# Attention values and row sums of two steps taken together at odd steps, in a fused macaron layer on eight cores

## What is computed

```python
x = x + 0.5 * ffn(layernorm(x))
x = x + attention(layernorm(x))      # 16 heads of 64, causal
x = x + 0.5 * ffn(layernorm(x))
```

```python
q = (x @ Wq.T + bq); k = (x @ Wk.T + bk); v = (x @ Wv.T + bv)
att = softmax(where(causal, q @ k.T / 8, -inf))
y = (att @ v) @ Wp.T + bp
```

## Time and profile before

| what | us |
|---|---|
| median of the runs shown | 1458.96 |
| the profiled execution | 1457.06 |
| its span, slowest core (core 4) | 1455.3 |
| spans of the 8 cores | 1439.4 to 1455.3 |
| TensorE busy (matmul) | 1227.4 |
| VectorE, ScalarE, GpSimd busy | 800.4, 712.0, 436.3 |

### The profile page before, as it was taken

The page is one execution under the profiler, slowest core; times in us unless marked ns, Lnnn a source line. Parts: engine busy times, 40 slices in busy tenths (PEclk is TensorE's granted clock), DMA queues, the critical chain, the costliest instruction groups (busy, mean ns, idle before and its releaser), DMA issues.

```text
span 1455.3 us, 27013 instructions; the slowest of 8 cores (1439.4 to 1455.3 us)
## 1 busy us (share of the span) xinstructions
PE 1227.4 (84%) x8256; PEld 475.0 (33%) x8392; DVE 800.4 (55%) x1469; ACT 712.0 (49%) x865; POOL 436.3 (30%) x308
## 2 busy tenths in 40 slices
PE   0338788879989999999999999966989799998977
PEld 0124333423333333333333333322333333333333
DVE  4466757646745745644654654425655445555545
ACT  0004335045646566566666566644646465565600
POOL 2012504503502412321340433324243232523222
PEclk9969999989999999999999999988999999999988
DMA  6828935146134324433433254243243343433132
GB/s 188 273 74 266 293 116 166 48 130 189 45 105 127 125 70 152 131 95 105 134 104 105 80 138 125 88 142 116 84 149 117 123 147 137 153 129 126 68 114 87
DMA packets 125929, 187.92 MB, mean 129 GB/s; under 512 B 45536, under 2 KB 90592, under 8 KB 125792
## 3 DMA queue, kind: packets, MB, share of 16 engines
q1 hardware_dynamic: 125792, 186.20, 40.3%
HBM read 119.05 MB, written 67.11 MB: 128 GB/s over the span
## 4 chain that ended last, share of the span: by engine, by line
PE 70%; DVE 10%; DMA 8%; issue 7%; ACT 2%; POOL 1%; SPq 1%; DVEq 0%; ACTq 0%; POOLq 0%
PE PS L689 14%; PE PS L702 13%; PE PS L619 10%; PE PS L638 10%; PE PS L744 7%; PE PS L712 7%; PE PS L646 6%; PE PS L667 3%; DMA WQKV<-x1d 2%; DVE XN L791 1%; DMA ATT<-wte 1%; DVE BNS L761 1%; DMA WQKV<-od 1%; PE PS L733 1%; DVE XT L807 1%
## 5 line engine op out<-in xcount | busy, mean ns | idle before, releaser
L930 ACT ACTIVATE PT<-PS,MB 128x1024 bf16<-128x1024 f32 (+3 forms) x428 | 401.3, 989 | 245.4 <-PE PS L619 245.4
L689 PE MATMUL PS<-WF,XT 128*128 128x512 bf16 x982 | 239.1, 391 | 31.2 <-DVE GD L813 23.5
L930 ACT ACTIVATE ATT<-PS,MB 128x1024 bf16<-128x1024 f32 x212 | 193.8, 965 | 123.3 <-PE PS L619 123.3
L702 PE MATMUL PS<-XT,WQKV 128*128 128x512 bf16 x979 | 233.5, 382 | 17.2 <-DVE QKS L847 7.5
L489 POOL TENSOR_TENSOR SQ<-QKS 128x512 bf16<-128x512 bf16 x128 | 143.9, 1127 | 291.0 <-DVE QKS L847 221.3
L619 PE MATMUL PS<-ATT 64*128 64x512 bf16 (+3 forms) x1280 | 185.6, 354 | 28.8 <-DMA ATT<-vd 17.1
L496 POOL TENSOR_TENSOR OTT<-OS,RR 128x512 bf16<-128x512 f32 x64 | 84.7, 1324 | 389.0 <-ACT RR L942 389.0
L744 PE MATMUL PS<-WP,WQKV 128*128 128x512 bf16 x490 | 126.0, 405 | 28.7 <-DMA WQKV<-od 18.0
L689 PEld LDWEIGHTS PS<-WF,XT 128*128 128x128 bf16 x1024 | 94.7, 100 | 151.2 <-issue 58.7
L702 PEld LDWEIGHTS PS<-XT,WQKV 128*128 128x128 bf16 x1024 | 91.8, 98 | 130.3 <-issue 36.4
L667 PE MATMUL PS<-IDE,XN 128*128 128x128 bf16 x768 | 63.7, 234 | 80.0 <-DVE XN L791 57.8
(11 more groups left out here) (75 smaller groups left out, 1200.8 us busy)
## 6 DMA issues: line engine op xcount, KB each, us to landing
XC<-x SPq DMA_DIRECT2D x32, 512.0 KB, 5.9
x1d<-XC SPq DMA_DIRECT2D x32, 512.0 KB, 4.6
WQKV<-x1d SPq DMA_DIRECT2D x32, 512.0 KB, 5.9
out<-WQKV SPq DMA_DIRECT2D x32, 512.0 KB, 3.3
qd<-QKS SPq DMA_DIRECT2D x64, 128.0 KB, 2.4
kd<-QKS SPq DMA_DIRECT2D x64, 128.0 KB, 2.1
vd<-VST SPq DMA_DIRECT2D x32, 256.0 KB, 2.7
ATT<-qd SPq DMA_DIRECT2D x64, 128.0 KB, 2.5
```

The lines of the kernel that those rows point to most:

```text
L689: m = e.matmul(sbank(en), x[:, dc, t * 128:(t + 1) * 128], WF[:, dc, h * 512:(h + 1) * 512], start=(dc == 0), stop=(dc == DCN - 1))
L702: m = e.matmul(sbank(en), WQKV[:, int(w), dc, hp * 128:(hp + 1) * 128], XT2[:, i % 2, dc, :], start=(dc == 0), stop=(dc == DCN - 1))
L930: e.activation(ptile(k)[:, 2 * m:2 * m + 2, off:512], PS[:, S_BANK + 2 * m:S_BANK + 2 * m + 2, off:512], AF.Exp, bias=MB[:, u // HPN, hp % ...
```

## The change

- `values(k)` works for two steps, k and k+1: eight value products, then eight row-sum products, and counts both at once (`then_inc(p_pv, 2)`). It is called at odd steps alone, behind `scores(k)`, for steps k-3 and k-2 (LAG = 3). Behind the scores of an even step nothing of the attention stands on TensorE.
- There are four buffers of exponentials instead of three: two in `PT`, two behind the ring. The exponential of step k waits for the values of step k-4.
- To make room, the ring shrinks from 10240 to 9216 columns, and the buffer `LNR` goes: the logarithm is written to `RR` and the exponential works there in place. So the wait for GpSimd's product of unit u-2 now stands ahead of the logarithm.
- Loads are entered in the order by what has been finished, and `PRED` follows from the smaller ring.

The core of the diff:

```diff
-LAG = 2
+LAG = 3
...
-RING = 10240
+RING = 9216
...
-        while u < NUNIT and START[u + 1] <= state["avail"] and START[PRED[u] + 1] <= max(0, state["k"] - LAG):
+        while u < NUNIT and START[u + 1] <= state["avail"] and START[PRED[u] + 1] <= state["done"]:
...
-        v = k - LAG
+        v = k - LAG + 1 if k % 2 and k > LAG - 2 else -1
+        if v >= 0:
+            state["done"] = v + 1
...
-            if k % 3 < 2:
-                return PT[:, k % 3, :, :]
-            return ATT[:, RING:RING + 2048].rearrange("p (a f) -> p a f", a=4)
+            if k % 4 < 2:
+                return PT[:, k % 4, :, :]
+            b = RING + 2048 * (k % 4 - 2)
+            return ATT[:, b:b + 2048].rearrange("p (a f) -> p a f", a=4)
...
             def values(k):
-                e.wait_ge(a_ex, 2 * k + 2)
-                if is_diag(k):
-                    e.wait_ge(v_mk, DIAG[k + 1])
+                e.wait_ge(a_ex, 2 * k + 4)
+                if is_diag(k + 1):
+                    e.wait_ge(v_mk, DIAG[k + 2])
                 if j == 0 and u:
                     e.wait_ge(v_oe, u)
-                for m in range(2):
+                for m in range(4):
...
-                                 vv[:, v + 64 * h:v + 64 * h + 64], ptile(k)[:, 2 * m + h, off:512],
+                                 vv[:, (j + m) * 128 + 64 * h:(j + m) * 128 + 64 * h + 64],
+                                 ptile(k + m // 2)[:, 2 * (m % 2) + h, off:512],
...
-                i.then_inc(p_pv, 1)
+                i.then_inc(p_pv, 2)
...
-                    if LAG <= k < NQUAD + LAG:
+                    if k % 2 and LAG <= k < NQUAD + LAG:
                         values(k - LAG)
...
-                        if k > LAG:
-                            e.wait_ge(p_pv, k - LAG)
+                        if k >= 4:
+                            e.wait_ge(p_pv, k - 3)
...
-                    if u:
-                        e.wait_ge(a_rc, u)
-                    was_read(e.activation(LNR[:, :], sbank(en), AF.Ln), en)
-                    read_out(e, en)
                     if u >= 2:
                         e.wait_ge(g_ot, u - 1)
-                    e.activation(RR[:, u % 2, :], LNR[:, :], AF.Exp, scale=-1.0).then_inc(a_rc, 1)
+                    x = RR[:, u % 2, :]
+                    was_read(e.activation(x, sbank(en), AF.Ln), en)
+                    read_out(e, en)
+                    e.activation(x, x, AF.Exp, scale=-1.0).then_inc(a_rc, 1)
```

More of the change, by code:

```diff
@@ L188, in make_order @@
     out = []
-    state = {"k": 0, "avail": 0, "acc": 0.0, "al": 0, "before": 0}
+    state = {"k": 0, "avail": 0, "acc": 0.0, "al": 0, "before": 0, "done": 0}
     def loads():
         u = state["al"]
-        while u < NUNIT and START[u + 1] <= state["avail"] and START[PRED[u] + 1] <= max(0, state["k"] - LAG):
+        while u < NUNIT and START[u + 1] <= state["avail"] and START[PRED[u] + 1] <= state["done"]:
             out.append(("al", u))
@@ L320, in build_program @@
         BD = sb("BD", [128, 2, 32], BF16)
-        ATT = sb("ATT", [128, NST * 2 * D], BF16)
+        ATT = sb("ATT", [128, RING + 4096], BF16)
         PT = sb("PT", [128, 2, 4, 512], BF16)
@@ L325, in build_program @@
         DSB = sb("DSB", [128, 2, 512], BF16)
-        LNR = sb("LNR", [128, 512], F32)
         RR = sb("RR", [128, 2, 512], F32)
@@ L359, in build_program @@
             "p (n m) f -> p n (m f)", n=NXC)
-        STG = ATT[:, :].bitcast(F32).rearrange("p (n f) -> p n f", n=NST)
+        STG = ATT[:, 0:NST * 2 * D].bitcast(F32).rearrange("p (n f) -> p n f", n=NST)
         BST = XT2[:, :, :, :].bitcast(F32).rearrange("p a c f -> p (a c f)").rearrange("p (n f) -> p n f", n=4)
@@ L628, in values @@
                 vv = vtile(u)
-                e.wait_ge(a_ex, 2 * k + 2)
-                if is_diag(k):
-                    e.wait_ge(v_mk, DIAG[k + 1])
+                e.wait_ge(a_ex, 2 * k + 4)
+                if is_diag(k + 1):
+                    e.wait_ge(v_mk, DIAG[k + 2])
                 if j == 0 and u:
                     e.wait_ge(v_oe, u)
-                for m in range(2):
+                for m in range(4):
                     off = k_off(c, j + m)
-                    v = (j + m) * 128
                     for h in range(2):
                         e.matmul(PS[64 * h:64 * h + 64, O_BANK, off:512],
-                                 vv[:, v + 64 * h:v + 64 * h + 64], ptile(k)[:, 2 * m + h, off:512],
+                                 vv[:, (j + m) * 128 + 64 * h:(j + m) * 128 + 64 * h + 64],
+                                 ptile(k + m // 2)[:, 2 * (m % 2) + h, off:512],
                                  start=(j + m == 0), stop=(j + m == end))
-                for m in range(2):
+                for m in range(4):
                     off = k_off(c, j + m)
                     for h in range(2):
-                        g = 2 * h + (m if c else 0)
+                        g = 2 * h + (m % 2 if c else 0)
                         i = e.matmul(PS[32 * g:32 * g + 32, D_BANK, off:512], ONES[:, 0:32],
-                                     ptile(k)[:, 2 * m + h, off:512],
-                                     start=(j == 0 and (m == 0 or c > 0)),
+                                     ptile(k + m // 2)[:, 2 * (m % 2) + h, off:512],
+                                     start=(j == 0 and (m == 0 or c > 0 and m == 1)),
                                      stop=(j + m >= end - (1 if c else 0)))
-                i.then_inc(p_pv, 1)
+                i.then_inc(p_pv, 2)
             for en in ORDER:
```

## The result

The changed kernel takes 1488.63 us (median; the kernel before 1457.01 beside it), 1.0208 times the kernel before, with a 95% interval from 1.0152 to 1.0265. On a later chip the same kernel gave 1.0185 (1.0132 to 1.0238). Each kernel has some runs in which the cores of a die show a lower granted clock and the time is longer (1609.85 and 1609.54 us here); they are in the medians, but not in the ratios and intervals. So the change is slower by about 2%, 27 to 30 us by the two ratios; whether by more or less than 2% the intervals leave open, as the forecast did (0.49 for slower, 0.47 for no change). 1489 us had been forecast. The experiments ran on three chips; the kernel before, which ran beside them each time, had medians of 1456.75 to 1459.96 us there.

A forecast was written before the change was run, and what follows sets the result against it. TensorE was taken to set the pace, with exponentials hidden by little. Terms -29 + 39 + 6 + 10 + 3 + 5 - 5 + 3 = +32 us on 1457 gave 1489 us; range 1463 to 1508, 8 times in 10.

The forecast's parts named there:

- The 45 and 15 steps behind a normaliser (+39, +6): Even steps right behind a unit's normaliser: scores wait for exponentials, 0.87 us at 45 (+39), some 0.4 at 15 (+6).
- Plain steps (+10, +3): Even steps with one projection: waits for exponentials, 0.21 us at 47 (+10), 0.12 at 24 with 384-wide second pair (+3).
- The saved changes of shape (-29): TensorE's values and row sums: 0.88 us removed from even steps, 0.70 added to odd, 0.18 saved a pair, times 160.
- Six steps without projection, and odd steps that fill waits (+5, -5): Values that hid in waits come later at 6 even steps (+5); longer batch fills waits at some 15 odd (-5).
- What was costed at nothing: Four buffers, the logarithm's earlier wait and the smaller ring: 0 us, at most 4 once for unit 48's loads.
- The clock: Rival: new waits bring stretches at a lower TensorE clock, adding 26 us, 1515 us; chance 6 in 100.
- Cover holds: Rival: TensorE never waits at the odd steps, only the saved changes of shape remain, 1428 us; chance 6 in 100.
- Waits half as large: Rival: normaliser steps partly covered by waits on banks and transposes, row sums join at 0.22, 1465 us; chance 25 in 100.
- The joined row sums cost more: Rival: second row-sum set starts only 0.33 us after the first, -29 shrinks by 14, 1503 us; chance 8 in 100.
- the rule on weight loads: Weight loads overlap a running matmul only for another group of rows; by it -29 would become +22, the time 1540.
- a term of 3 us for other steps alone: 23 even steps with more work, no normaliser: projection may reach its bank before VectorE has read it; +3, between 0 and 8.
- a sign of being wrong: The projection behind even scores starting much later than 0.53 us after them.

The follow-up runs named there:

- the first edit: The changed kernel with each unit's broadcast, logarithm and exponential of the normaliser one projection later, ahead of an odd step: 1424.77 us, ratio 0.9776.
- half the dose: The changed kernel with a shorter normaliser in place (logarithm and nearly all of the second exponential left out, layer not computed): 1471.22 us in the profiled execution.
- the move alone: The kernel before, without the change, with the normaliser shifted one projection later: 1461.37 us, ratio 1.0018.
- the late normaliser: The changed kernel with the normaliser one projection later, the same kernel as the first edit: 1424.77 us, ratio 0.9776; on another chip 1438.01 us, ratio 0.9843.
- the values ahead of the scores: The changed kernel with the odd step's batch of values and row sums ahead of its scores, normaliser in place: 1453.54 us, ratio 0.9963.
- the batch undone: The changed kernel with values and row sums of the two steps done one step after the other inside the odd step: 1521.98 us, ratio 1.0419.

## Why the prediction came out right

- **The sum.** +32 us forecast, +27.6 in mean span, +26 in the profiled executions (1482.72 against 1457.06), +30 by the ratio. The mechanism was the one forecast: the time is lost where the exponentials behind a normaliser are no longer covered.
- **The 45 and 15 steps behind a normaliser (+39, +6).** Right in place, mechanism and size. Forecast +2.74 and +3.74 for the two pairs, measured +2.69 and +3.70; the first edit got the time back, half the dose a part of it, and the move alone nothing in the kernel before. Most of the first pair's delay is the bank wait, though, which is not in the forecast of +2.74. The 15 steps shortened less than I had put: 13 us of work was removed and 3.9 us saved, where 7 were expected.
- **Plain steps (+10, +3).** Right. The median length of a plain full step is 2.58 us where scores and projection take 2.37; of one with a 384 wide second pair it is 2.37, where 2.26 would do (the next pair follows 0.11 sooner).
- **The saved changes of shape (-29).** Right in kind, too small. What I put at 0.46 us for two pairs of value products is 0.43 (0.98 against 0.55), the second set of row sums took 0.22, not 0.24, and the projection after scores started after 0.54, as assumed. So 0.88 - 0.65 = 0.23 us a full pair, up to 37 us; undoing the batch cost 33. The 143 odd steps with one projection grew by 93.5 us, which is 0.65 each.
- **Six steps without projection, and odd steps that fill waits (+5, -5).** The first class kept its length to 0.1 us, as said. The second came true too: the 14 odd steps without a projection grew by 4.0 us where 14 times 0.65 is 9.1, so waits took up 5. That the odd steps' sum grew by 10 us less than expected is owed to the term above.
- **What was costed at nothing.** The memory part cost nothing that can be measured, by its own run. Unit 48's last load was issued at 975.87, landed at 980.26 and was used at 984.01, 3.7 us to spare; 1 to 2 had been forecast.
- **The clock.** It was to stay at 1.00 from 560 to 910 us; it was 0.99. An estimate from that is 7 us of 350 at the lower level of 1.2 GHz, which costs at most half as much. Over the whole span the mean of the eight cores went from 0.961 to 0.956, by which at most 8 us of TensorE's time were lost, an estimate too; the late normaliser had 0.959 and 0.954 on its two chips. This rival came true in a small part, a few us:

```profile
619.00:692.00 73.00, 67.02 (x480) 24.77 (x476) 36.04 (x72) 43.62 (x51) 16.86 (x11) 0.98 0.31 93
...
560.00:910.00 350.00, 322.91 (x2250) 123.63 (x2248) 184.06 (x348) 209.38 (x252) 98.06 (x78) 0.99 0.36 113
```

- **The rivals.** "Cover holds" fell with 34.3 us of waits. "Waits half as large" was right that the row sums join at 0.22, and wrong on the waits: the 60 steps gave back all but 5 of their 53 us. "The joined row sums cost more" fell, and the rule on weight loads that the prediction took from the Trainium skill fell for row sums too: they joined at 0.22, not 0.33.
- **A missing term.** The bank wait of 0.3 us of the projection behind a broadcast was in my list as a term of 3 us for other steps alone, and under the larger wait it did no harm. Behind a broadcast the projection started 0.83 us after the scores, which I had named as a sign of being wrong. The same omission made the forecast for the values ahead of the scores miss by 25 us. The agreement of the sum to a few us is partly luck: the odd steps came out 10 us cheaper than forecast, nearly all of it the value products and row sums that join sooner, and against it the three larger kinds of even steps kept 7 us more than forecast.

## What to carry to other kernels

Work that is moved off a waiting pair of engines is also cover that is taken away: add up, for each gap, what the slower partner has to do in it, including what stands ahead of it in its queue only every few rounds. Here a wait of 0.9 us at 45 places and a shorter one at 15 lay hidden behind 0.88 us of products and stood in no list of waits before. When gaps become uneven, put the rare extra work into the long gap, and look at when it gives back the bank that it holds: here this made 3.5 to 4.4% between two orders of the same instructions (ratios 1.0185 and 0.9843, 1.0208 and 0.9776).

## What the runs showed of the hardware

A change of TensorE's array shape between products of 512 columns cost 0.09 to 0.12 us: 0.31 us from the last product of one shape to the first of the next (scores to values, 0.53 less 0.22), where products of one shape follow at 0.22, and 0.12 each in the batch undone. Eight row-sum products on four column groups, two sets on the same columns, took 0.55 us to the next projection (745.04 to 745.59), four alone 0.33 (758.98 to 759.31), so a second set costs 0.22, the distance of two products, and no time of its weight load shows. The score products that waited for ScalarE started 0.14 us after the exponential's end, as at 713.76 before the change.
